# A convolution layer and a Mamba layer on one core: the Mamba's chunk grows from 512 to 1024 steps, in units that hold 64 channels and two time halves

## The chip, the core and the metric

The kernel runs on one core of a Trainium2 chip. A core has a matrix engine (PE, also called TensorE, with its weight loads shown apart as PEld), three engines for elementwise work (DVE, ACT and POOL), a queue that issues DMAs (SP), a working memory of 128 partitions (SBUF) and a small accumulation memory that PE writes (PSUM). The metric is the time of the program on the device in microseconds (us); lower is better. Each engine runs its own list of instructions in the order in which the program wrote them, and engines wait for each other through semaphores.

## What is computed

The input is 16 samples of 64 x 64 positions with 96 channels. Layer 0 normalizes, upsamples by a Fourier series, applies two dense layers with a polynomial between them, filters and downsamples, and is added to its input. Layer 1 normalizes and applies a Mamba block to the 4096 positions of a sample as one sequence; it too is added to its input. Cut to the Mamba:

```python
xz = einsum('blc,ec->ble', u, W_in); xs, z = split(xz, 2)        # 192 channels each
xc = silu(sum(xp[:, k:k + L, :] * conv_w[:, k] for k in range(3)) + conv_b)
dbc = einsum('bld,ed->ble', xc, W_x)                             # dt (6), B (16), C (16)
delta = softplus(einsum('blr,dr->bld', dt, W_dt) + b_dt)
dA  = exp(delta[..., None] * A)                                  # 192 channels x 16 states
dBu = delta[..., None] * Bm[:, :, None, :] * xc[..., None]
# for each step t:  h = dA_t * h + dBu_t ;  y_t = sum over states of h * C_t
y = (ys + xc * D) * silu(z)
out = einsum('bld,cd->blc', y, W_out)
```

Everything is float32, but for B, which is split into three bfloat16 parts that PE adds up again.

## The kernel before

The samples form a pipeline. While the Mamba works on sample s, the engines also do the steps of layer 0 for later samples: "S" steps (statistics and the first resampling), "W" steps (upsampling W_up, dense layers W_f and W_2, downsampling W_dn) and "D" steps (the last resampling, which also gives the input of the Mamba). A planner (`level`, `even`, `stage_rows`, with PE costs in `PE_US`) spreads these steps over the slots of a sample, and every engine's program is then written slot by slot by `run`: first the Mamba's unit of that slot, then its smaller parts, then the layer 0 steps that are due, each engine some slots behind PE (`LAG`). The order is fixed when the program is built. All layer 0 steps and the Mamba's own matrix steps (X, Z, DBC, DT, OUT) share three PSUM banks in turn (`cb`, `RING`).

The Mamba goes through a sample in 8 chunks of T = 512 steps. The recurrence runs on 128 partitions, which hold 32 channels times 4 states. A chunk thus has 24 units (6 groups j of 32 channels, 4 groups q of states), and a unit is one slot. For each unit:

- ACT makes `av` = exp(A x delta) from `rep_d` (L1008); `rep_d` and `rep_u` are delta and delta x xc, copied four times over the partitions by DMA from DRAM scratch.
- PE spreads B of one state group over the partitions into the bank `pb` (`spread_b`, L846), once for three units.
- DVE multiplies three strips of `rep_u` with `pb` into three PSUM banks `b3` (L1134), and then scans the three units one by one (L1140): `hs` = av x h + b.
- POOL multiplies `hs` with C, `cs` (L1181), and keeps the last state (L1185).
- PE adds up the four states of a channel into `py`, three strips of 32 partitions at once (`reduce`, L855).

After four state groups ACT copies `py` out (L1051), and POOL adds xc x D and multiplies with silu(z) (L1230, L1233). A chunk later PE makes OUT from that (`out`, L837 and L838). Two chunks ahead (`LEAD` = 2) the inputs are prepared: X (the convolution as three matmuls on shifted data, L810), Z (L816), DBC (L820), DT (L825), ACT's silu and softplus, the delta store to DRAM, POOL's multiply delta x xc (L1218), the deltax store, and the loads of `rep_d`, `rep_u` and `cs`. The table `AT` says in which slot of a chunk each part stands. WARM (L710) are matmuls without use that `warm` places in groups of slots with little PE work.

The broadcast for the next three units waits for DVE's multiply, since `pb` is a single buffer; DVE's multiply waits for the scans before it, since `b3` is:

```python
pe.wait_ge(dve_bu, count(dve_bu, G * NG + g))      # spread_b, PE
dve.wait_ge(pe_b, count(pe_b, G * NG + g + 1))     # unit, DVE: the multiply
dve.wait_ge(dve_h, count(dve_h, G * NU + n))
```

Of the kernel before, what the change touches and what calls it, by code (L numbers as in the profile page):

```python
# [13 lines left out]
L = HH * WW  # L14
# [7 lines left out]
T = 512  # L22
NC8 = L // T
NJ, NQ = DI // 32, DSTATE // 4
NU = NJ * NQ
NG = NU // 3
NHC, NAV, NHS = 6, 8, 6
XB_H = 8
LEAD = 2
# [4 lines left out]
BATCH = 8  # L34
# [8 lines left out]
LAG = {"pe": 0, "act": 4, "dve": 3, "pool": 1, "sp": 1, "bn": 3}  # L43
UNRINGED = ("SLD", "WLD", "DLD", "DW", "WARM")
# [24 lines left out]
def d_steps():  # L69
# [4 lines left out]
S_LAST, W_FIRST, W_LAST, D_FIRST, D_LAST = 87, 105, 87, 100, 139  # L74
X_AT, Z_AT, DBC_AT, DT_AT = (8, 10), (12, 11), 14, 18
KEEP_FREE = tuple(range(9, 9))

PE_US = {"ST": 0.45, "SA": 0.70, "SB": 0.70, "W_up": 0.70, "W_f": 0.71, "W_2": 2.10, "W_dn": 0.75, "D_lo": 1.20, "D_hi": 1.20,
         "X": 2.72, "Z": 0.92, "DBC": 1.82, "DT": 0.50, "OUT": 2.70, "WARM": 0.215}
PE_PB, PE_RED = 0.22, 1.00  # L80

WARM_TO = 4.8
# [4 lines left out]
def even(steps, lo, hi):  # L87
    free = [p for p in range(lo, hi + 1) if p % NU not in KEEP_FREE]
    return [(free[i * len(free) // len(steps)], st) for i, st in enumerate(steps)]


def loads(lo, hi, rows):

    load = {}
    for p in range(lo, hi + 1):
        load[p] = PE_PB * (p % 3 == AT["pe"]["pb"]) + PE_RED * ((p - AT["pe"]["red"]) % 3 == 0)
    for p, st in rows:
        if lo <= p <= hi:
            load[p] += PE_US.get(st[0], 0.2)
    return load  # L100


def level(steps, lo, hi, rows):
# [3 lines left out]
    for p in range(lo, hi + 1):  # L107
        groups.setdefault((p - 1) // 3, []).append(p)
    for limit in range(300, 1200, 5):
        out, todo = [], list(steps)  # L110
        for slots in groups.values():
            room = limit / 100 * len(slots) / 3 - sum(load[p] for p in slots)
            share = room / len(slots)
            for i, p in enumerate(slots):
                while (todo and p % NU not in KEEP_FREE and room >= PE_US[todo[0][0]] / 2
# [8 lines left out]
def warm(rows):  # L124
    load = loads(0, NC8 * NU - 1, rows)
    out = []
    for p in range(3, NC8 * NU, 3):
        short = WARM_TO - load[p] - load[p - 1] - load[p - 2]
        out += [(p, ("WARM", p, i)) for i in range(int(short / PE_US["WARM"]))]
    return out  # L130


def mamba_rows(k, z_only=False):
    at = k * NU
    rows = [(at + Z_AT[t], ("Z", k, t)) for t in range(2)]
    if not z_only:
        rows += [(at + X_AT[t], ("X", k, t)) for t in range(2)] + [(at + DBC_AT, ("DBC", k))]
        rows += [(at + DT_AT, ("DT", k, t)) for t in range(2)]
    return rows


def stage_rows(s, w_head, w_tail, d, beside=()):
# [20 lines left out]
def plan_of(kind):  # L163
    rows = []
    for k in range(NC8):
        if kind != "last" or k < NC8 - LEAD:
            rows += mamba_rows(k)
        elif k == NC8 - LEAD:
            rows += mamba_rows(k, True)
        rows.append((k * NU + OUT_AT, ("PAD", -1) if kind == "first" and k == 0 else ("OUT", k)))  # L170
    if kind == "last":
        rows.append((NC8 * NU + OUT_AT, ("OUT", NC8)))
        return padded(rows)
    rows = stage_rows(kind != "tail", kind != "tail", True, True, rows) + rows
# [1129 lines left out]
```

## Time and profile before

| | |
|---|---|
| median of 3 runs | 6343.44 us (6342.52 to 6347.34) |
| profiled execution, span from its first to its last instruction | 6343.7 us |
| PE busy, DVE busy, POOL busy, ACT busy | 6036.5, 5685.5, 5209.8, 5097.3 us |
| DVE scans (3072) | 3257.8 + 466.9 us |
| DVE multiplies (1024) | 1803.5 us |
| POOL multiplies with C (3072) | 3835.6 us |

The first 330 us prepare the first sample; from then on the recurrence runs without a break to the end, 16 samples after each other. The last two samples have less layer 0 work beside them. Busy time is not the same as being the bound: an engine may be busy with work for which nobody waits. The rows that say who waits for whom stand below.

### The profile page before, as it was taken

To read this page: it belongs to the slowest core of one execution; us is meant where nothing else is said; L and a number is where in the kernel's file an instruction comes from. 1 tells how busy PE (TensorE), PEld (TensorE's weight loads), DVE (VectorE), ACT (ScalarE), POOL (GpSimd) and SP (SyncE) were. 2 spreads that over 40 slices of the span, in tenths; PEclk is the share of its full clock that TensorE was granted. 3 is DMA by queue.
4 is the path that set the end of the run, shared out by engine and by line. 5 is a ranking of instruction groups with operands and counts; after the bars stand their busy time and mean duration, and the time that the engine had idled before them with its cause. 6 is when DMAs were issued, how large, how long until landed. Compare 5 with 4: busy or idle time off the path is not lost. (4 is left out here: it accounts for less than half of the span.)

```text
span 6343.7 us, 99100 instructions
## 1 busy us (share of the span) xinstructions
PE 6036.5 (95%) x32260; PEld 3123.0 (49%) x32260; DVE 5685.5 (90%) x4459; ACT 5097.3 (80%) x8658; POOL 5209.8 (82%) x5092
## 2 busy tenths in 40 slices
PE   8999999999999999999999999999999999998776
PEld 5645445454554545545455544545455454554222
DVE  0089999999999999999999999999999999999998
ACT  4588888888888888888888788888888888887664
POOL 0078888888888888888888888888888888888988
PEclk9999999999999999999999999999999999998665
DMA  3367676676767667675676767667676766767553
GB/s 95 88 165 170 160 167 157 163 162 169 169 154 168 155 165 170 155 182 142 167 162 162 173 156 169 155 164 163 167 169 156 166 154 165 168 142 160 129 124 75
DMA packets 805826, 983.25 MB, mean 155 GB/s; under 512 B 391258, under 2 KB 417542, under 8 KB 805318
## 3 DMA queue, kind: packets, MB, share of 16 engines
q1 hardware_dynamic: 805318, 976.92, 65.4%
q8 instruction: 265, 4.34, 0.3%
q14 instruction: 243, 1.99, 0.1%
HBM read 717.71 MB, written 259.00 MB: 154 GB/s over the span
## 5 line engine op out<-in xcount | busy, mean ns | idle before, releaser
L1181 POOL TENSOR_TENSOR hc<-hs,cs 128x512 f32<-128x512 f32 x3072 | 3835.6, 1271 | 692.7 <-DVE hs L1140 505.6
L1140 DVE TENSOR_TENSOR_SCAN hs<-av,state,b 128x512 f32<-128x512 f32 x2688 | 3257.8, 1263 | 88.6 <-POOL state L1185 4.9
L1008 ACT ACTIVATE av<-rep_d,nega 128x512 f32<-128x512 f32 x3072 | 2096.7, 713 | 41.5 <-DVE hs L1140 36.8
L1134 DVE TENSOR_TENSOR b<-rep_u,pb 128x1536 f32<-128x1536 f32 x1024 | 1803.5, 1761 | 211.0 <-PE pb L846 124.7
L855 PE MATMUL py<-hc,rsel 128*32 128x512 f32 x6144 | 1141.6, 634 | 40.6 <-POOL hc L1181 39.7
L769 PE MATMUL cb<-xu,w1a 96*128 96x392 f32 x2400 | 984.3, 513 | 27.7 <-DVE b1a L1120 17.4
L774 PEld LDWEIGHTS cb<-w2c,g 128*98 128x98 f32 x9600 | 885.9, 167 | 169.7 <-issue 106.9
L774 PE MATMUL cb<-w2c,g 128*98 128x96 f32 x9600 | 910.7, 252 | 17.4 <-ACT g L956 9.3
L956 ACT ACTIVATE g<-cb,b1a 128x392 f32<-128x392 f32 x1200 | 679.5, 579 | 87.0 <-PE cb L769 78.8
L810 PE MATMUL cb<-xn,wtap 96*96 96x512 f32 x1536 | 723.3, 607 | 2.4 <-ACT xn L1029 2.4
L769 PEld LDWEIGHTS cb<-xu,w1a 96*128 96x128 f32 x2400 | 414.5, 191 | 415.4 <-issue 199.3
L846 PE MATMUL pb<-bc,selb 96*128 96x512 bf16 x1024 | 406.6, 397 | 140.5 <-DVE b L1134 140.4
L1140 DVE TENSOR_TENSOR_SCAN hs<-av,zero_state,b 128x512 f32<-128x512 f32 x384 | 466.9, 1264 | 11.8
L949 ACT ACTIVATE vr<-cb 98x384 f32<-98x384 f32 x400 | 194.9, 487 | 320.2 <-PE cb L774 318.2
L810 PEld LDWEIGHTS cb<-xn,wtap 96*96 96x96 f32 x1536 | 243.5, 166 | 400.4 <-issue 380.0
L855 PEld LDWEIGHTS py<-hc,rsel 128*32 128x32 f32 x6144 | 157.2, 110 | 455.7 <-POOL hc L1181 225.0
L1218 POOL TENSOR_TENSOR dlt<-dlt,xcs 96x1024 f32<-96x1024 f32 x128 | 301.8, 2358 | 68.5 <-DMA delta_scratch<-dlt 68.5
L846 PEld LDWEIGHTS pb<-bc,selb 96*128 96x128 bf16 x1024 | 103.7, 101 | 508.1 <-issue 246.3
L763 PE MATMUL cb<-up_h,t1r 128*96 128x196 f32 x1600 | 345.7, 339 | 7.7 <-DMA t1r<-t_scratch 7.5
L837 PE MATMUL cb<-wo,xcs 96*128 96x96 f32 x2048 | 341.0, 292 | 3.7 <-POOL xcs L1233 3.5
L1233 POOL TENSOR_TENSOR xcs<-xcs,zs 96x512 f32<-96x512 f32 x256 | 324.1, 1266 | 20.1
L837 PEld LDWEIGHTS cb<-wo,xcs 96*128 96x128 f32 x2048 | 291.5, 205 | 86.0 <-issue 49.5
(109 smaller groups left out, 6703.4 us busy)
## 6 DMA issues: line engine op xcount, KB each, us to landing
rep_d<-delta_scratch SPq DMA_DIRECT2D x512, 384.0 KB, 7.0
rep_u<-deltax_scratch SPq DMA_DIRECT2D x512, 384.0 KB, 6.3
cs<-c_scratch SPq DMA_DIRECT2D x512, 256.0 KB, 5.9
delta_scratch<-dlt SPq DMA_DIRECT2D x128, 384.0 KB, 3.1
deltax_scratch<-dlt SPq DMA_DIRECT2D x128, 384.0 KB, 9.2
t1r<-t_scratch SPq DMA_DIRECT2D x160, 240.0 KB, 6.5
v_scratch<-v2s SPq DMA_DIRECT2D x192, 192.0 KB
xb<-in_x SPq DMA_DIRECT2D x128, 192.0 KB, 4.6
```

What stands on the lines that cost most here:

```text
L763: mm = pe.matmul(bank[0:C, e * 2 * GH:(e + 1) * 2 * GH], t1r[:, m % 2, i2 % 5, :], up_h[:, :], start=True, stop=True)
L769: mm = pe.matmul(bank[:, 0:BC], w1a[:, 128 * f:128 * f + 128], xu[:, b % 2, :], start=True, stop=True)
L774: mm = pe.matmul(bank[0:GH, C * j:C * j + C], g2[:, b % 2, f, GH * j:GH * j + GH], w2c[:, f, :], start=(f == 0), stop=(f == NF - 1))
L810: mm = pe.matmul(bank[0:C, :], wtap[:, tap, t, :], xn[:, k2 % 2, tap:tap + T], start=(tap == 0), stop=(tap == 2))
L837: pe.matmul(o, xcs[:, p, t, tb], wo[:, t, :], start=(t == 0), stop=False)
L846: pe.matmul(pb[:, :], selb[:, g % NQ, :], bc3[:, k % 4, :], start=True, stop=True).then_inc(pe_b, 1)
L855: mm = pe.matmul(py[32 * j:32 * j + 32, :], rsel[:, :], hc[:, (3 * g + j) % NHC, :], start=(q == 0), stop=(q == NQ - 1), skip_group_check= ...
L956: act.activation(g2[:, b % 2, f, :], bank[:, 0:BC], ACT.Square, bias=b1a[:, f:f + 1]).then_inc(fr, 1)
L1008: act.activation(av[:, n % NAV, :], rep_d[:, k % 2, j, :], ACT.Exp, scale=nega[:, q, j:j + 1])\
L1134: dve.tensor_tensor(b3[:, :, :], rep_u[:, k % 2, 3 * hf:3 * hf + 3, :], pb[:, None, :].broadcast_to([128, 3, T]), ALU.mult).then_inc(dve_b ...
L1140: dve.tensor_tensor_scan(hs[:, n % NHS, :], av[:, n % NAV, :], b3[:, n % 3, :], start, ALU.mult, ALU.add)\
L1181: pool.tensor_tensor(hc[:, n % NHC, :], hs[:, n % NHS, :], cs[:, k % 2, g % NQ, :], ALU.mult)\
```

## The change

The Mamba now goes in chunks of 1024 steps, four to a sample, and prepares one chunk ahead (`LEAD` = 1). A tile of prepared data (xc, z, delta, y) has 64 channels on each half of the partitions: steps 0 to 511 of the chunk on partitions 0 to 63, steps 512 to 1023 on partitions 64 to 127. There are three such tiles instead of two of 96 channels. X, Z and DT are now two matmuls side by side in the columns of PE's array, one for each time half; DBC, OUT and B's broadcast are two matmuls side by side in its rows. In the recurrence a unit still holds 32 channels times 4 states, but 1024 steps, so there are 24 units to 1024 steps in place of 48, and a unit takes two slots.

B's broadcast goes into `ub`, two buffers of 1024 steps, once for each unit, and DVE multiplies `rep_u` into it in place, unit by unit. The sum over states adds four strips at once (two units, two time halves). WARM is gone. `rep_d` and `rep_u` are loaded in three jobs a chunk of two units' data each, `cs` in four, one for each state group, with a single buffer. The rings of `av`, `hs` and `hc` hold four units of 1024 steps in place of 8, 6 and 6 of 512.

```diff
-T = 512
-NC8 = L // T
+TC = 512
+T = 2 * TC
...
-NHC, NAV, NHS = 6, 8, 6
+NHC, NAV, NHS = 4, 4, 4
-LEAD = 2
+LEAD = 1
...
-OUT_AT = 20
+OUT_AT = 9
 AT = {
-    "pe": dict(pb=1, red=5),
-    "act": dict(xn=10, y=(18, 6), d=11, mid=23, batch=16),
+    "pe": dict(red=6),
+    "act": dict(xn=5, d=10, batch=17, delta=27, mid=30, fin=36, y=(24, 40, 8)),
     "dve": dict(),
-    "pool": dict(u=23, bc=(18, 22), y=(17, 8)),
-    "sp": dict(rd=(1, 2, 3, 4), ru=(7, 9, 11, 13), cs=(15, 16, 17, 18), dl=21, du=4, x1=21, out=23),
+    "pool": dict(bc=(24, 30), u=32, y=(20, 36, 4)),
+    "sp": dict(x1=1, dc=23, dl=29, du=36, out=18, rd=((33, 0), (46, 0), (13, 1)), ru=((39, 0), (2, 1), (17, 1)),
+               cs=((40, 0), (44, 0), (47, 0), (3, 1))),
 }
...
-X_AT, Z_AT, DBC_AT, DT_AT = (8, 10), (12, 11), 14, 18
+Z_AT, X_AT, DBC_AT, DT_AT = (12, 13, 14), (9, 10, 11), 18, (22, 23, 24)
...
+            def spread_b(G, u):
+                if u == 0:
+                    pe.wait_ge(act_bc, count(act_bc, G + 1))
+                pe.wait_ge(dve_h, count(dve_h, G * NU + u - 1))
+                for h in range(2):
+                    part = slice(64 * h, 64 * h + 48)
+                    mm = pe.matmul(ub[:, u % 2, TC * h:TC * h + TC], selb[part, u // 2 % NQ, :], bc3[part, G % 2, :],
+                                   start=True, stop=True)
+                mm.then_inc(pe_b, 1)
...
+            def reduce(G, g):
+                t, q = g // NQ, g % NQ
+                pe.wait_ge(pool_hc, count(pool_hc, G * NU + 2 * g + 2))
+                if q == 0:
+                    pe.wait_ge(act_y, count(act_y, G * NP + t))
+                for h in range(2):
+                    for j in range(2):
+                        strip = 32 * (2 * h + j)
+                        mm = pe.matmul(py[strip:strip + 32, :], rsel[:, :], hc[:, (2 * g + j) % NHC, TC * h:TC * h + TC],
+                                       start=(q == 0), stop=(q == NQ - 1), skip_group_check=True)
+                mm.then_inc(pe_red, 1)
...
+                dve.wait_ge(pe_b, count(pe_b, G * NU + u + 1))
+                dve.tensor_tensor(ub[:, u % 2, :], rep_u[:, jobs % 2, u % 2, :], ub[:, u % 2, :], ALU.mult)\
+                    .then_inc(dve_bu, 1)
+                if u % 2 == 0:
+                    dve.wait_ge(pool_st, count(pool_st, G * NG + u // 2 + 1 - NHS // 2))
+                dve.wait_ge(dve_bu, count(dve_bu, G * NU + u + 1))
+                dve.wait_ge(act_a, count(act_a, G * NU + u + 1))
```

On PE, in the middle of a chunk before, around the two X steps: `pb` is B's broadcast, `cb<-xn,wtap` X, `cb<-xn,winz` Z, `py` the sum over states, `xb` and `vr` belong to layer 0.

```order
L846 MATMUL pb<-bc,selb 128x512
L855 MATMUL py<-hc,rsel 32x512 x3
L742 MATMUL cb<-xb,up_w 100x384
L810 MATMUL cb<-xn,wtap 96x512 x3
L846 MATMUL pb<-bc,selb 128x512
L810 MATMUL cb<-xn,wtap 96x512 x3
L855 MATMUL py<-hc,rsel 32x512 x3
L816 MATMUL cb<-xn,winz 96x512
L742 MATMUL cb<-xb,up_w 100x384
L816 MATMUL cb<-xn,winz 96x512
L846 MATMUL pb<-bc,selb 128x512
```

The same place after the change; ahead of these rows stand the broadcast for unit 5 (`ub`) and three more quarters of OUT (`cb<-wo,xcs` and `cb<-ident,x1o`), each like the first two rows:

```order
L886 MATMUL cb<-wo,xcs 128x96 x6
L890 MATMUL cb<-ident,x1o 128x96 x2
L846 MATMUL cb<-xn,wtap 64x512 x6
L915 MATMUL py<-hc,rsel 32x512 x4
L846 MATMUL cb<-xn,wtap 64x512 x6
L903 MATMUL ub<-bc,selb 128x512 x2
L776 MATMUL cb<-xb,up_w 100x384
L846 MATMUL cb<-xn,wtap 64x512 x6
L797 MATMUL cb<-up_h,t1r 96x196 x2
L854 MATMUL cb<-xn,winz 64x512 x2
L903 MATMUL ub<-bc,selb 128x512 x2
```

OUT, which stood ten slots behind the X steps, now stands directly ahead of them, and the broadcasts of units 6 and 7 stand between the second and third X and behind the first Z.

On DVE, at the border of two chunks before (`b` is the product of rep_u and B, `hs` the scan, `spare` belongs to a filling step):

```order
L1140 SCALAR_TENSOR_TENSOR hs<-av,state,b 128x512 [waits act_a,dve_bu,pool_st]
L1140 SCALAR_TENSOR_TENSOR hs<-av,state,b 128x512 [waits act_a] x2
L1100 COPY spare<-cb 96x1 [waits pe_conv]
L1134 TENSOR_TENSOR b<-rep_u,pb 128x1536 [waits dve_h,pe_b,ru_ld0]
L1140 SCALAR_TENSOR_TENSOR hs<-av,zero_state,b 128x512 [waits act_a,dve_bu,pool_st]
```

The same place after the change:

```order
L1177 COPY spare<-cb 96x1 [waits pe_conv]
L1210 TENSOR_TENSOR ub<-rep_u,ub 128x1024 [waits pe_b,ru_ld0]
L1217 SCALAR_TENSOR_TENSOR hs<-av,zero_state,ub 128x1024 [waits act_a,dve_bu,pool_st]
L1210 TENSOR_TENSOR ub<-rep_u,ub 128x1024 [waits pe_b]
L1217 SCALAR_TENSOR_TENSOR hs<-av,zero_state,ub 128x1024 [waits act_a,dve_bu]
```

Multiply and scan now alternate, each multiply waits for PE's broadcast (pe_b), and none waits for the scans before it (dve_h).

On SP, where the transfers for a coming chunk are issued, before (`x1c` is the input of X and Z, `rep_u`, `rep_d` and `cs` feed the recurrence):

```order
L659 DMA rep_d<-delta_scratch 32x6x512
L513 DMA t1r<-t_scratch 128x5x96 [waits pe_conv]
L662 DMA rep_u<-deltax_scratch 32x6x512 [waits du_st,dve_bu]
L662 DMA rep_u<-deltax_scratch 32x6x512 x3
L576 DMA v_scratch<-v2s 2x64x384 [waits cb_free1]
L666 DMA cs<-c_scratch 32x4x512 [waits dc_st,pool_hc]
L666 DMA cs<-c_scratch 32x4x512 x3
L605 DMA x1c<-x_scratch 96x512 [waits x1_st0,x1_st1,act_xn]
```

After (`xn` is now loaded directly):

```order
L666 DMA rep_u<-deltax_scratch 32x2x1024 [waits du_st,dve_bu]
L666 DMA rep_u<-deltax_scratch 32x2x1024 x3
L585 DMA v_scratch<-v2s 2x64x384 [waits cb_free2]
L698 DMA cs<-c_scratch 32x1024 [waits dc_st,pool_hc]
L698 DMA cs<-c_scratch 32x1024 x3
L698 DMA cs<-c_scratch 32x1024 [waits dc_st,pool_hc]
L698 DMA cs<-c_scratch 32x1024 x3
L522 DMA t1r<-t_scratch 128x5x96 [waits pe_conv]
L666 DMA rep_d<-delta_scratch 32x2x1024 [waits dl_st,act_a]
L666 DMA rep_d<-delta_scratch 32x2x1024 x3
L698 DMA cs<-c_scratch 32x1024 [waits dc_st,pool_hc]
L698 DMA cs<-c_scratch 32x1024 x3
```

The next row after these is the load of `xn`; the first `rep_u` here is that of the chunk which begins next, where before it was that of the chunk after next.

## Rows read from the trace of the kernel before

**Rows 1.** The page: span, busy time and share of each engine.

```profile
span 6343.7 us, 99100 instructions
...
PE 6036.5 (95%) x32260; PEld 3123.0 (49%) x32260; DVE 5685.5 (90%) x4459; ACT 5097.3 (80%) x8658; POOL 5209.8 (82%) x5092
```

**Rows 2.** 375 us in mid-run: busy PE, PEld, DVE, ACT, POOL; granted clock, DMA share, GB/s.

```profile
1083.00:1458.00 375.00, 368.34 (x2016) 191.28 (x2015) 354.01 (x278) 316.20 (x541) 325.05 (x318) 1.00 0.70 164
```

**Rows 3.** DVE in order of time: start, length, line, operation, count.

```profile
2505.96 1.76 DVE L1134 TENSOR_TENSOR b<-rep_u,pb 128x1536 f32<-128x1536 f32 x1
2507.81 3.63 DVE L1140 TENSOR_TENSOR_SCAN hs<-av,state,b 128x512 f32<-128x512 f32 x3
2511.54 1.76 DVE L1134 TENSOR_TENSOR b<-rep_u,pb 128x1536 f32<-128x1536 f32 x1
```

**Rows 4.** DVE's waits: total us, times, longest us.

```profile
DVE b L1134 <- PE pb L846: 124.7, 182, 3.4
```

**Rows 5.** Scans: shortest/median/longest ns, first and last start in us.

```profile
L1140 DVE TENSOR_TENSOR_SCAN hs<-av,state,b x2688: 1248/1256/1283, 386.9 to 6326.3; 128x512 f32<-128x512 f32 x192
L1140 DVE TENSOR_TENSOR_SCAN hs<-av,zero_state,b x384: 1248/1256/1282, 330.0 to 6013.6; 128x512 f32<-128x512 f32 x192
```

**Rows 6.** Groups by line: busy us, mean ns of one | idle before, releaser.

```profile
L1113 DVE BATCH_NORM_STATS2 bst<-x1s 96x6 f32<-96x512 f32 x128 | 85.3, 666 | 51.7 <-ACT x1s L965 51.7
```

**Rows 7.** The same view, POOL's multiplies of 512 and of 1024 steps.

```profile
L1230 POOL TENSOR_TENSOR xcs<-xcs,yv 96x512 f32<-96x512 f32 x256 | 325.8, 1273 | 2.7 <-ACT yv L1051 2.7
L1218 POOL TENSOR_TENSOR dlt<-dlt,xcs 96x1024 f32<-96x1024 f32 x128 | 301.8, 2358 | 68.5 <-DMA delta_scratch<-dlt 68.5
```

**Rows 8.** PE in order of time around X; a matmul counts as two half passes.

```profile
2518.79 2.74 PE L810 MATMUL cb<-xn,wtap 96*96 96x512 f32 x6
2521.37 0.38 PE L846 MATMUL pb<-bc,selb 96*128 96x512 bf16 x1
2521.58 2.74 PE L810 MATMUL cb<-xn,wtap 96*96 96x512 f32 x6
2524.25 1.06 PE L855 MATMUL py<-hc,rsel 128*32 128x512 f32 x6
2525.24 2.26 PE L816 MATMUL cb<-xn,winz 96*96 96x512 f32 x4
```

**Rows 9.** PE in order of time around one W_dn.

```profile
2504.05 0.87 PE L780 MATMUL cb<-vr,dn_h 98*64 98x384 f32 x4
2504.84 0.33 PE L747 MATMUL cb<-mv,gavg 96*96 96x1 f32 x2
```

**Rows 10.** PE in order of time: OUT's first row and what follows it.

```profile
2497.23 0.61 PE L837 MATMUL cb<-wo,xcs 96*128 96x96 f32 x4
...
2499.91 0.38 PE L846 MATMUL pb<-bc,selb 96*128 96x512 bf16 x1
```

**Rows 11.** SP: four issues, DMAs with KB and us to landing, one wait.

```profile
2519.80 2.64 SPq L662 DMA_DIRECT2D rep_u<-deltax_scratch  x4
...
rep_u<-deltax_scratch SPq DMA_DIRECT2D x512, 384.0 KB, 6.3
delta_scratch<-dlt SPq DMA_DIRECT2D x128, 384.0 KB, 3.1
deltax_scratch<-dlt SPq DMA_DIRECT2D x128, 384.0 KB, 9.2
...
SPq L648 <- DMA deltax_scratch<-dlt: 432.1, 86, 9.0
```

**Rows 12.** WARM matmuls; the last sample's stretch; PE in it, in order.

```profile
L710 PE MATMUL py<-selb 96*32 96x512 bf16 x673 | 160.2, 381 | 0.0
...
5964.00:6327.00 363.00, 259.07 (x818) 88.17 (x817) 350.14 (x262) 217.17 (x326) 322.29 (x315) 0.62 0.47 108
...
6052.70 1.17 PE L837 MATMUL cb<-wo,xcs 96*128 96x96 f32 x4
...
6057.93 0.63 PE L846 MATMUL pb<-bc,selb 96*128 96x512 bf16 x1
```

More of the change, by code:

```diff
@@ L87, in even @@
 def even(steps, lo, hi):
-    free = [p for p in range(lo, hi + 1) if p % NU not in KEEP_FREE]
+    free = list(range(lo, hi + 1))
     return [(free[i * len(free) // len(steps)], st) for i, st in enumerate(steps)]
@@ L121, in level, with mamba_rows @@
     raise ValueError("the steps find no place")
[L124 to L138, printed above, removed]
+def mamba_rows(k, z=True, ahead=True):
+    at = k * NS2
+    rows = []
+    if ahead:
+        rows += [(at + X_AT[t], ("X", k, t)) for t in range(NP)]
+    if z:
+        rows += [(at + Z_AT[t], ("Z", k, t)) for t in range(NP)]
+    if ahead:
+        rows += [(at + DBC_AT, ("DBC", k, h)) for h in range(2)]
+        rows += [(at + DT_AT[t], ("DT", k, t)) for t in range(NP)]
     return rows
@@ L152, in stage_rows @@
         rows += [(S_LAST + 4, ("WLD", 0)), (W_FIRST - 3, ("WG", 0))] + even(w[:2], W_FIRST - 8, W_FIRST - 6)
-        rows += level(w[2:W_HEAD], W_FIRST, NC8 * NU - 1, rows + list(beside))
+        rows += level(w[2:W_HEAD], W_FIRST, SL - 1, rows + list(beside))
     return rows
@@ L456, in iteration @@
                 for k in chunks:
-                    for n in range(NU):
-                        if units and k < NC8:
+                    for n in range(NS2):
+                        if units and k < NC:
                             unit_fn(st.s, k, n)
                         c_fn(st, k, n)
-                        if not (last and k + LEAD >= NC8):
+                        if not (last and k + LEAD >= NC):
                             a_fn(st, k, n)
-                        while todo and when(todo[0]) <= k * NU + n:
+                        while todo and when(todo[0]) <= k * NS2 + n:
                             step_fn(st, todo.pop(0)[1])
@@ L675, in c_part @@
+                if n == at["out"] and not (G < 1):
+                    k1, s1 = (k - 1) % NC, st.s + (k - 1) // NC
+                    for h in range(2):
+                        i = st.at[("OUT", k, h)]
+                        sp.wait_ge(cb_free[i % RING], st.freed(i))
+                        sp.sem_inc(sp_passed, 1)
+                        sp.dma_start(tok(otok, s1, k1 * T + h * TC, TC), os_[:, h]).then_inc(out_st, 16)
+                if n == at["out"] and k < NC and not (G < 0):
                     load_x1o(st.s, k)
@@ L877, in _ @@
+                late = n + NS2 - AT["pe"]["red"]
+                if late < NS2 and late % 4 == 0 and not (G < 1):
+                    reduce(G - 1, late // 4)
             run(lambda row: row[0], unit, step, lambda st, k, n: None, c_part, setup)
```

622 lines of the change are left out of this document (325 added, 297 removed).

## The prediction

> **What bounds the kernel now.** I began with the page: PE is busy 95% of the span, DVE 90% [rows 1]. A busy PE need not be the bound, so I cut whole samples out of the middle: in 375 us DVE works 354, PE 368, at a granted clock of 1.00 [rows 2]. DVE's order of time decides between the two: one multiply of 1536 steps, three scans, the next multiply 5.58 us after the last (1.76 + 0.09 + 3.63 + 0.10), with no wait inside [rows 3]. So DVE's own work is the floor. Its list of waits names the one thing that lifts time above it: the multiply waits 124.7 us for PE's broadcast of B [rows 4]. The execution adds up: first scan at 330.0, last one over at 6326.3 + 1.3 = 6327.6 [rows 5]; between them 1024 x 5.58 = 5714 of floor, 124.7 of waiting, 159 of statistics and small things (the rest; the statistics alone are 0.67 us each, rows of one kind x128 [rows 6]); then 16.1 to the end. Sum 6343.7, the span, and the median of the runs is 6343.44, so a sum against the span needs no correction.
>
> **DVE's new floor.** A unit is now 1024 steps: one multiply and one scan. No row has these lengths, so each price has two ends. Multiply: two thirds of 1.76 are 1.17; and between statistics over 512 elements at 0.67 [rows 6] and the multiply over 1536 at 1.76 lie 1024 elements and 1.09 us, so 512 fewer make 1.21. I take 1.23, since statistics write next to nothing. Scan: two thirds of three scans' 3.63 are 2.42 [rows 3]; one scan of double length saves the start between two, about 0.1, so 2.33, at most 2.43. The gap between multiply and scan stays at 0.09, since the scan waits for its own multiply as before. The gap behind the scan should go: the multiply no longer waits for the scan before it (the order shows no dve_h on it), and three scans without such a wait last 3.63 instead of 3 x 1.26, an overlap of 0.08 at each of two borders [rows 3, 5]. I take 1.23 + 0.09 + 2.33 - 0.08 = 3.57, with ends 3.50 (multiply 1.17) and 3.85 (scan 2.43, gap of 0.10 kept; less what the pile below then loses, 390 us more). 1536 x 3.57 = 5484, which is 230 less than 5714. With 330, 159 and 16.1 unchanged (head and tail keep their steps but for some tiny loads) the sum without waits is 5989.
>
> **What the change takes from other engines** lies beside DVE and I count it at nothing. ACT and POOL lose per-instruction starts (POOL's 1024-step form is 2.36, two of 512 are 2.54 [rows 7]); ACT is busy 80% of the span and POOL 82% [rows 1]. PE loses work: per 1024 steps, X goes from 12 passes of 0.86 to 9 pairs, the sums from 16 of 1.0 to 12, Z, DBC and DT from 4 passes to 3 pairs, while the broadcast grows from 16 single matmuls to 24 pairs [rows 8]. This holds if pairs on separate column halves run together; they do so now in W_dn, where four half passes of 384 columns take 0.79 us to the next instruction, against 4 x 0.32 one by one (an X half pass of 512 takes 0.43 [rows 8, 9]). So PE is lighter on average. Average is not what ends a wait here.
>
> **Where the floor is lost: the pile on PE.** B's broadcast for unit u+1 goes into the buffer in which unit u-1's product stood, so PE may write it only when scan u-1 is over, and DVE needs it when unit u is over. Between two broadcasts PE therefore has at most two units, 7.14 us. Before, OUT and the two X stood apart, with a broadcast between any two of them. Now the order shows between the broadcasts of units 5 and 6, in every chunk: OUT for 1024 steps, X, a sum, X. Count from the chunk's first multiply. Scan 3 is over at 4 x 3.57 = 14.3, the broadcast of unit 5 takes 0.3 (0.21 from [rows 8], and about 0.1 for the change of tile shape: the sum's two passes of 0.43 take 0.99 there). OUT also waits for the last third of y: POOL does it behind the product of unit 2, that is 10.7 + 2.36 + 1.27 + 1.27 = 15.6 [rows 7]. OUT before is 2.69 for 24 half passes, 0.112 each [rows 10]; now 64. If the two halves of rows go together that is 40 x 0.112 = 4.5, if not 64 x 0.112 = 7.2; no row shows row halves, the column halves of [rows 9] speak for together, and I take 5.0. Then X 2.6, sum 1.0, X 2.6, broadcast 0.3 [rows 8]: 15.6 + 11.5 = 27.1. DVE has been done with unit 5 since 21.4. **Stall 5.7 us.** Before the next broadcast stand the third X, W_up (0.7: four half passes of 196 columns at X's rate) and Z (0.86): 2.6 + 0.7 + 0.86 + 0.3 = 4.5 against 3.57, 0.9 more; then PE is level. 6.6 us a chunk, in 63 of 64 chunks: **416 us**. Ends: 4.2 (OUT 4.5, no wait for y, no second stall) and 8.8 (OUT 7.2): 265 to 554.
>
> The row says that a change of tile shape costs about 0.1 us. The Trainium skill, in TensorEngine Tiling (Array Packing), Key Properties, states that changing the tiling mode drains the TensorE; it speaks against this change, in which nearly every PE instruction stands beside one of another shape. Row and rule agree; without the pile's five such borders the sum would be 63 x 0.5 = 30 us lower, 6500.
>
> **Other waits.** The 124.7 us before come from groups in which PE is a little late; elsewhere PE has 6 to 7 us of work in each two units by the order, so I keep half, 62 (0 to 125). **Transfers:** product and next chunk now lie within one chunk. The deltax store can go when POOL has multiplied three times behind unit 17, at about 70 us; it then lands in 3.1 (what the delta store takes) to 9.2, four issues take 2.6 and rep_u lands in 6.3 [rows 11]: 82 to 88, and unit 24 begins at 85.7. (The stall above moves both alike.) Behind it in SP's queue stand cs, rep_d, cs, and only then xn, for which ACT waits ahead of its next exponentials; today's queue has SP waiting 432 us for the deltax store without hurting DVE, because that store is a chunk ahead [rows 11]. I take 1 us a chunk, 63 (0 to 4 each, 252).
>
> **Sum:** 5989 + 416 + 62 + 63 = **6530**, 2.9% above 6343.7. No change would need all waits together at 355, 5.6 a chunk.
>
> **Rivals.**
> *The floor wins (faster).* If OUT's two row halves hide each other's weight loads too, OUT for 1024 steps costs the 2.7 of one OUT before, y is ready by then, and the broadcast of unit 6 is done at 14.6 + 2.7 + 2.6 + 1.0 + 2.6 + 0.3 = 23.8 against 21.4: 2.5 a chunk, 5989 + 158 + 62 = 6209. For it: pairs of column halves do run together [rows 9]. Against: 64 half passes must then take the time of 24, and X alone twice is 5.2 of 7.14. It decides below 5.6 a chunk.
> *PE's clock falls (slower).* The filler matmuls are gone; before there were 673 of them, and in the stretch without them the clock was 0.62 of full (half speed, 1.2 GHz, for much of it), OUT took 5.23 instead of 2.69 [rows 12]. If each pile begins at half speed, OUT's 40 steps cost 40/24 x 2.54 = 4.2 more: 6530 + 63 x 4.2 = 6795. For it: four groups with little PE work ahead of one of the four piles. Against: three of four piles follow dense work. The Trainium skill names this in TensorE: Matmul & The Clock Gate, HAM oscillation: waits between bursts of matmuls bring the lower clock back. The row of the last stretch agrees.
> *Late transfers (slower).* 4 us a chunk instead of 1: 6719.
> *In place costs double (slower).* The multiply reads and writes one PSUM bank, which no row shows; before it read one and wrote another. At half rate it costs 1.07 more: 1536 x 1.07 = 1643, less 63 x 2.1 at the pile: 8040.
> *The change doesn't do what it says (slower).* If four strips don't run together as three do, each of 768 sums takes 1.9 instead of 1.0, and PE, already near 7 us per two units, becomes the bound; with a fifth of it finding room, 6530 + 0.8 x 768 x 0.9 = 7080.
>
> **How the numbers follow.** Forecast 0.63, floor 0.16, clock 0.06, transfers 0.08, in place 0.04, strips 0.03. Within 0.2% is about what measurement can tell from no change. Of the forecast's 0.63 its low end gives 0.02 to faster and 0.03 to same; the floor rival is faster throughout. Faster 0.18, same 0.03, slower 0.79. Range 6220 to 6820: below it lies some 0.10 (most of the floor rival), above it some 0.11 (in place, strips, the top of the forecast).
>
> **What would show it.** Right: DVE's waits put 300 to 500 us on the multiply for PE, nearly all on units 6 and 7 of each chunk; multiply near 1.23, scan near 2.33, pairs of them 3.57 apart elsewhere; OUT 4.5 to 5.5 us long. Wrong: the multiply well over 1.3 (in place), sums over 1.1 (strips), a granted clock below 0.95 in mid-sample (clock), DVE waiting for rep_u or av (transfers), or DVE's waits for PE under 200 us (the floor wins).

## The result, and the profile after

The changed kernel takes **7996.47 us** (median of 4 runs, 7967.36 to 8004.99) against 6342.98 before: a ratio of 1.2597, interval 1.2574 to 1.2621. Slower, as forecast, but the forecast was 6530 and its range ended at 6820. The profiled execution spans 8001.2 us. The runs of this kernel lie within 38 us of each other, so in the experiments, which are single runs, a smaller difference says nothing.

The page: no engine is busy all the time any more, PE least of all compared with [rows 1], and its granted clock (tenths of full, 40 slices) is below 9 nearly everywhere.

```profile
span 8001.2 us, 101956 instructions
...
PE 6590.0 (82%) x36195; PEld 3216.6 (40%) x36195; DVE 5568.4 (70%) x3441; ACT 4513.5 (56%) x6604; POOL 4596.4 (57%) x3108
...
PEclk9888978788797887878789788887978888787555
```

The groups of DVE and of the sum (count | busy us, mean ns | idle before, releasers):

```profile
L1210 DVE TENSOR_TENSOR ub<-rep_u,ub 128x1024 f32<-128x1024 f32 x1536 | 1867.8, 1216 | 2037.0 <-PE ub L903 1963.5 <-DMA rep_u<-deltax_scratch 71.1
L1217 DVE TENSOR_TENSOR_SCAN hs<-av,state,ub 128x1024 f32<-128x1024 f32 x1152 | 2703.1, 2346 | 85.4 <-ACT av L1073 10.3 <-DVE ub L1210 2.2 <-issue 0.9
L915 PE MATMUL py<-hc,rsel 128*32 128x512 f32 x6144 | 1013.2, 738 | 408.7 <-POOL hc L1260 309.5 <-ACT yv L1122 95.7
```

DVE's instructions cost what was forecast (1.216 and 2.346 us; forecast 1.23 and 2.33). Nearly all the loss is one entry: the multiply waits 1963.5 us for PE's broadcast, where [rows 4] had 124.7 and the forecast 416 + 62. The lists of waits (us, times, longest) name a second one, on ACT, that the kernel before doesn't have:

```profile
DVE ub L1210 <- PE ub L903: 1963.5, 557, 18.0
...
ACT xn L1094 <- DMA xn<-x_scratch: 894.1, 63, 23.7
```

The four chunks of one sample (columns as in [rows 2]): DVE works 81 to 93 us in each, about its floor, and PE's clock is far from [rows 2]'s 1.00.

```profile
3253.00:3370.00 117.00, 102.54 (x570) 49.27 (x571) 87.12 (x55) 71.69 (x106) 71.31 (x47) 0.87 0.60 132
3370.00:3487.00 117.00, 92.38 (x507) 40.33 (x505) 86.15 (x53) 68.02 (x98) 72.01 (x49) 0.81 0.54 125
3487.00:3625.00 138.00, 113.82 (x612) 59.97 (x612) 93.23 (x62) 69.93 (x105) 74.48 (x51) 0.76 0.61 136
3625.00:3743.00 118.00, 103.19 (x574) 51.00 (x573) 81.09 (x47) 71.75 (x105) 69.55 (x47) 0.87 0.50 112
```

**Where in a chunk.** I took DVE's time between the end of a scan and the next multiply from the order of time (it includes the few statistics that stand there) and averaged it over the 56 chunks of the samples in the middle. Of 33.0 us a chunk, 14.0 stand ahead of units 2 to 4, 10.5 ahead of units 6 and 7 (7.4, 7.8, 19.2 and 7.7 in the four chunks of a sample), 5.2 ahead of units 12 to 15, 3.2 elsewhere. Only the second place was forecast, at 6.6.

The first place, in the second chunk of a sample, in order of time (ACT, PE, DVE):

```profile
3372.35 0.49 ACT L1010 ACTIVATE vr<-cb 98x384 f32<-98x384 f32 x1 [0.63 <-PE cb L808]
3386.47 0.20 ACT L1094 ACTIVATE xn<-xn 96x2 f32<-96x2 f32 x1 [13.63 <-DMA xn<-x_scratch]
...
3387.71 0.47 ACT L1010 ACTIVATE t1s<-cb 100x384 f32<-100x384 f32 x1
...
3375.36 0.93 PE L803 MATMUL cb<-xu,w1a 96*128 96x392 f32 x2
3388.23 1.60 PE L776 MATMUL cb<-xb,up_w 64*100 64x384 f32 x2 [11.95 <-ACT t1s L1010]
3389.76 2.98 PE L803 MATMUL cb<-xu,w1a 96*128 96x392 f32 x4
3392.67 0.61 PE L903 MATMUL ub<-bc,selb 48*128 48x512 bf16 x2
...
3378.84 2.35 DVE L1217 TENSOR_TENSOR_SCAN hs<-av,state,ub 128x1024 f32<-128x1024 f32 x1
3393.32 1.23 DVE L1210 TENSOR_TENSOR ub<-rep_u,ub 128x1024 f32<-128x1024 f32 x1 [12.14 <-PE ub L903]
```

ACT stands 13.63 us in front of xn. Behind that wait stands its eviction of t1s, for which PE waits 11.95 us, and when PE goes on it does so at half clock (0.93 us for two matmuls before, 2.98 for four after). DVE has waited 12.14 us when the broadcast comes. The second place in the third chunk, on PE: OUT (L886, L890), X (L846), the sum, one D step, X, and the broadcast that DVE waits for.

```profile
3524.09 0.91 PE L886 MATMUL cb<-wo,xcs 64*128 64x96 f32 x12 [2.26 <-issue]
...
3530.80 1.60 PE L886 MATMUL cb<-wo,xcs 64*128 64x96 f32 x12
3532.33 1.17 PE L890 MATMUL cb<-ident,x1o 96*128 96x96 f32 x4
3533.43 5.39 PE L846 MATMUL cb<-xn,wtap 96*64 96x512 f32 x12
3538.75 1.26 PE L915 MATMUL py<-hc,rsel 128*32 128x512 f32 x8
...
3541.22 2.80 PE L846 MATMUL cb<-xn,wtap 96*64 96x512 f32 x12
3543.95 0.39 PE L903 MATMUL ub<-bc,selb 48*128 48x512 bf16 x2
```

The same quarter of OUT takes 0.91 and 1.60 us, the same X 5.39 and 2.80: half clock for some 13 of the 20 us. And OUT begins late: over the samples in the middle 3.7 us behind the multiply of unit 4, against 0.0 to 0.6 in the other three chunks. PE stands 2.26 us in front of it, until 0.09 us after DVE's small step `b1a`, which reads one of the shared banks and has its place behind a scan in DVE's list.

### The profile page after: what moved, and what is told of

Its sections match the earlier page's. It is cut to its first block and busy times, and to the rows that moved or that the text cites. A ratio compares the mean times of both kernels' runs of the same rounds, so it can differ in the third digit from the quotient of the medians.

```text
span 8001.2 us, 101956 instructions
## 1 busy us (share of the span) xinstructions
PE 6590.0 (82%) x36195; PEld 3216.6 (40%) x36195; DVE 5568.4 (70%) x3441; ACT 4513.5 (56%) x6604; POOL 4596.4 (57%) x3108
## 5 line engine op out<-in xcount | busy, mean ns | idle before, releaser
L1260 POOL TENSOR_TENSOR hc<-hs,cs 128x1024 f32<-128x1024 f32 x1536 | 3618.6, 2356 | 2583.5 <-DVE hs L1217 2530.7
L1210 DVE TENSOR_TENSOR ub<-rep_u,ub 128x1024 f32<-128x1024 f32 x1536 | 1867.8, 1216 | 2037.0 <-PE ub L903 1963.5
L1217 DVE TENSOR_TENSOR_SCAN hs<-av,state,ub 128x1024 f32<-128x1024 f32 x1152 | 2703.1, 2346 | 85.4 <-ACT av L1073 10.3
L1073 ACT ACTIVATE av<-rep_d,nega 128x1024 f32<-128x1024 f32 x1536 | 1736.8, 1142 | 170.7 <-DVE hs L1217 168.1
L1217 DVE TENSOR_TENSOR_SCAN hs<-av,zero_state,ub 128x1024 f32<-128x1024 f32 x384 | 901.0, 2346 | 26.3 <-ACT av L1073 1.7
L903 PE MATMUL ub<-bc,selb 48*128 48x512 bf16 x3072 | 667.2, 433 | 163.6 <-DVE hs L1217 162.6
L846 PE MATMUL cb<-xn,wtap 96*64 96x512 f32 x2304 | 584.6, 646 | 0.0
L797 PEld LDWEIGHTS cb<-up_h,t1r 128*96 128x96 f32 x1600 | 258.3, 182 | 378.1 <-issue 195.9
L1289 POOL TENSOR_TENSOR xcs<-xcs,yv 128x512 f32<-128x512 f32 x192 | 243.5, 1268 | 279.9 <-ACT yv L1122 279.8
L886 PE MATMUL cb<-wo,xcs 64*128 64x96 f32 x3072 | 281.0, 326 | 32.6 <-issue 27.7
```

Of the source, the lines that this page charges most:

```text
L797: mm = pe.matmul(bank[0:C, e * 2 * GH:(e + 1) * 2 * GH], t1r[:, m % 2, i2 % 5, :], up_h[:, :], start=True, stop=True)
L846: mm = pe.matmul(bank[64 * h:64 * h + 64, :], wtap[:, tap, :, :].rearrange("c t p -> c (t p)")[:, own], xn[:, G2 % 2, TC * h + tap:TC * h ...
L886: pe.matmul(cb[:, (i + h) % RING, C * b:C * b + C], xcs[half, (G - 1) % 2, j, 128 * b:128 * b + 128], wo[half, j, :], start=(j == 0), stop ...
L903: mm = pe.matmul(ub[:, u % 2, TC * h:TC * h + TC], selb[part, u // 2 % NQ, :], bc3[part, G % 2, :], start=True, stop=True)
L1073: act.activation(av[:, u % NAV, :], rep_d[:, jobs % 2, j, :], ACT.Exp, scale=nega[:, q, at:at + 1])\
L1210: dve.tensor_tensor(ub[:, u % 2, :], rep_u[:, jobs % 2, u % 2, :], ub[:, u % 2, :], ALU.mult)\
```

## The experiments

Four theories stood at the start: **A**, the late load of xn; **B**, half clock; **C**, the pile of OUT and X, as forecast; **D**, ub released too late. **P** (PE has no room on average), **Q** (less work, more half clock) and **L** (lockstep) came later.

**e1: xn earlier.**

```diff
-                if n == at["x1"]:
+                if n == at["x1"] and G2 == 0:
                     load_xn(s2, k2)
+                if n == 45 and G2 + 1 < NS * NC:
+                    load_xn(*divmod(G2 + 1, NC))
```

> Only the load of xn is issued earlier: at slot 45 of the chunk before, ahead of the second rep_d job and the third cs job, instead of slot 1. Theory A (ACT stands in its queue before xn until the load lands, 63 waits of 14 us, 894.1 us in all; the evictions behind it are late, so PE and the broadcasts for units 2 to 4 are): DVE's idle time ahead of units 2 to 4, 13.9 us a chunk, goes almost whole, 63 x 13 = 820, so 7180 us, and up to 300 lower if PE then keeps its clock, so 6880 to 7200; ACT's wait for xn under 100 us. Theory B (PE at half clock is the cause, and the wait for xn only fills time that PE would lose anyway): the idle time moves on to units 6 and 7, 7700 us or more, and the clock stays near 0.82. Theory C (the pile of OUT and X is the cause, as forecast): at most the waits ahead of units 2 to 4 shrink by half, 7500 or more.

The time was 7622.06 us, and ACT's wait was still 393.1. Half of the wait went and 374 us with it: A has a share, but the time lies above its range, in that of C.

**e2: X, Z, DBC, DT and what follows two slots later** (`X_AT` = 11, 12, 13; `OUT_AT` stays 9).

> X, Z, DBC, DT and everything made from them stand two slots later, so that the broadcast of unit 6 lies between OUT and X. Theory A (late xn): X is not held up by the late load any less, the waits at units 2 to 4 stay at 14 us a chunk, only a part of the pile (units 6 and 7, 10.5 us a chunk) goes: 63 x 5 = 315, so 7680, between 7550 and 7850. Theory C (the pile): the 10.5 us at units 6 and 7 fall to 3 and the chain behind them catches up, 63 x 7.5 = 470 or more, 7520 or less. Theory B (half clock): 7850 to 8050, since PE's work is the same.

The time was 8159.56 us, above the range of every theory. Units 6 and 7 lost most of their wait outside the third chunk (0.4 to 0.6 and 2.0 to 2.6), but it came back at units 0, 3, 8 and 11. That speaks against C as stated.

**e3: product into hs, scan in place there; the broadcast waits for the multiply (dve_bu), not for the scan.**

> The product is written into hs and the scan runs in place there, so PE may write the next broadcast as soon as the multiply two units before is over, 2.4 us earlier than now. Theory D (the short release of ub is what makes DVE and PE wait for each other): every late broadcast gains up to 2.4 us; DVE's 557 waits for PE shrink by 2.4 each at most, 1300 us, and at least by PE's own waits for the scan, 162.6 us: 6700 to 7500. Theories A, B and C: waits of 7 to 18 us a piece are hardly shorter, 63 x 2 piles x 2.4 = 300, so 7600 to 7850. If the in-place form itself had cost the multiply or the scan anything, 1.22 and 2.35 us would fall; no theory here expects that.

The time was 8940.86 us: a scan took 3.19 us instead of 2.35, and POOL's copy of the state 1.65 instead of 0.19. All four theories missed this; it needed e7.

**e4: the kernel before without fillers** (`WARM_TO = 0.0`).

> The kernel before without its 673 filling matmuls (160 us of PE). Theory B (the fillers held the clock, and PE's clock falls without them whatever else is done): the granted clock falls below 0.90, DVE's waits for PE grow from 125 to 400 us or more, 6600 to 7000. Theories A, C and D (the clock falls in the changed kernel because PE stands idle behind ACT or in the ping-pong with DVE): the clock stays above 0.93 and the time within 6300 to 6420.

The time was 6355.15 beside 6350.33 us, and the clock 0.945 beside 0.966. In the kernel before, the fillers held up 0.02 of the clock and no time.

**e5: xn earlier still** (slot 36; 45 where the chunk begins a sample).

> The load of xn is issued at slot 36 of the chunk before (slot 45 only where the chunk begins a sample), 9 slots or some 17 us earlier than in the first experiment, where ACT still waited 393.1 us for it (6 us in two chunks of four, 14 in one). Theory A (what ACT waits for xn comes back in the time almost one to one): ACT's wait for xn under 100 us, 7622 - 300 = 7320, between 7200 and 7400. Theory AB (PE's idle time behind ACT also costs it the clock, so that every stall is paid twice): the share of half clock falls with it, granted clock over 0.90, 6900 to 7200. Theory P (PE's own work, 355 us a sample at full clock against DVE's 353, leaves no room, and PE's remaining waits and half clock come from its ping-pong with DVE): 7400 or more.

The time was 7568.07 us at clock 0.844, in the range of P; ACT's wait is 0.8 us in all. Taking the whole wait of 894 us away gives back 428. Units 2 to 4 fell from 14.0 to 5.6 us, and units 6 and 7 rose from 10.5 to 12.4: in the second chunk of a sample the 12 us ahead of unit 3 went, and 13.5 stand ahead of unit 6, where some 6 stood. There OUT now waits 1.4 us for POOL's last third of y, and then takes 9.8 us instead of 5.7, at half clock for much of it.

Other waits of PE come into view. Its list between 400 and 7000 us (over its whole span the kernel before has 29.1 for xb, 17.4 for b1a, 7.5 for t1r and none for xt):

```profile
PE cb L773 <- DMA xb<-in_x: 74.2, 13, 6.2
PE cb L888 <- DVE b1a L1199: 53.9, 14, 3.9
PE cb L830 <- DMA xt<-xt_scratch: 51.4, 15, 5.4
PE cb L799 <- DMA t1r<-t_scratch: 44.4, 14, 4.0
```

Three of the four are loads of layer 0 from the same SP queue. In one sample of e11 (below), which has them as well, PE waits 5.72 us for xb ahead of the broadcast for unit 3 in the first chunk, and 3.63 and 3.22 us for xt and t1r ahead of that for unit 2 in the third; DVE then waits 5.99 and 7.78 us. No run took these waits away.

**e6: the late load put into the kernel before** (`load_x1c` at slot 5 of its own chunk for every second chunk).

> The kernel before, with the load of the layer input x1c of every second chunk of 512 issued at slot 5 of the chunk that needs it, instead of slot 21 of the chunk before; nothing else. That puts the changed kernel's late load into the kernel before, 64 times. Theory A (a late load that ACT waits for stops PE and with it DVE): ACT waits 8 to 15 us each time, and since PE there works 368 us of 376, nearly all of it is seen: 64 x 7 to 64 x 13, 6790 to 7180. With theory AB the granted clock falls too (under 0.92, from 0.965) and it is 7000 to 7500. Rival: the kernel before is deeper (8 units of av ahead, prepared two chunks ahead) and takes it in: under 6500.

The time was 6550.15 us beside 6342.41. The waits:

```profile
ACT xn L1031 <- DMA x1c<-x_scratch: 206.1, 64, 9.3
```

ACT waits less than expected (3.2 us each), and the time lies between the two ranges. But 206 us of waiting cost 208 us: in this kernel A's price, one to one, is right, with the clock nearly unmoved (0.955 against 0.966).

**e7: product in an SBUF buffer of its own** (`bu`; the scan reads it there, and the broadcast waits as in e3).

```diff
...
+                dve.wait_ge(dve_h, count(dve_h, G * NU + u))
-                dve.tensor_tensor(ub[:, u % 2, :], rep_u[:, jobs % 2, u % 2, :], ub[:, u % 2, :], ALU.mult)\
+                dve.tensor_tensor(bu[:, :], rep_u[:, jobs % 2, u % 2, :], ub[:, u % 2, :], ALU.mult)\
...
```

> The product is written into a buffer of its own in SBUF, neither in place in PSUM (as changed) nor in place in SBUF (as in e3, where the scan took 3.19 us instead of 2.35 and GpSimd's products 2.64 instead of 2.36). PE may write the next broadcast once the multiply two units before is over, 2.35 us sooner than in the changed kernel. Theory S (a scan whose inputs both lie in SBUF gets in GpSimd's way and is slowed by it): scan 3.0 us or more, 8600 or more. Theory I (it was the scan in place in SBUF that was slow): scan 2.35 to 2.55, GpSimd at 2.36. With I, theory D (the late release of ub makes the waits) gives 7850 or less; if the release does not matter, 1536 scans that are 0.1 to 0.2 longer give 8000 to 8250.

The time was 8949.76 us. DVE and POOL, groups:

```profile
L1219 DVE TENSOR_TENSOR_SCAN hs<-av,state,bu 128x1024 f32<-128x1024 f32 x1152 | 3499.2, 3038 | 76.2 <-ACT av L1074 2.4 <-issue 1.3 <-DVE bu L1212 0.9
...
L1262 POOL TENSOR_TENSOR hc<-hs,cs 128x1024 f32<-128x1024 f32 x1536 | 4048.5, 2638 | 1922.3 <-DVE hs L1219 1921.9 <-PE py L916 0.4
L1265 POOL COPY state<-hs 128x2 f32<-128x2 f32 x768 | 1239.5, 1614 | 0.0
```

The scan is not in place, and as slow as in e3: S, not I. Scans with POOL at work for less than a fifth of their time take 2.36 us, the others 3.2 to 3.7 in the mean and up to 4.5. The Trainium skill, SBUF — State Buffer, "SBUF: two separate sides", says that VectorE with two SBUF inputs and GpSimd lock each other out of a port for a whole instruction if GpSimd's reads SBUF; these rows agree, as a scan of 2.36 us that grows to 4.5 has gained about one POOL product (2.36 us in the changed kernel). So e3 and e7 say nothing on D, which stays open; with one operand in PSUM, before and after, there is no such price.

**e8: e5 and e2 together.**

> The load of xn as in e5_xn36, and X, Z, DBC and DT two slots later as in e2, so that a broadcast stands between OUT and X. With the late load gone, theory C (the pile) gives back what stands ahead of units 6 and 7, 9 us a chunk, without the late load taking it again: 350 to 550 below e5_xn36. Theory P (PE is the bound on average, so a pile that is spread out is paid in small pieces elsewhere): within 150 of e5_xn36, either side.

The time was 7637.31 us, 69 more than e5. C as stated falls again, P stands.

**e9: less work on PE, away from the pile** (each W_2 adds one of its three products; the other two are left out).

> As e5_xn36, but each W_2 step adds one of its three products instead of all three: two thirds of layer 0's second matrix product are left out, and what the kernel writes changes accordingly. That takes 400 of 600 small matmuls a sample from PE, 400 x 92 ns = 37 us of its 355 us at full clock. None of them stands in the piles at units 3, 6 and 12. Theory P (PE's work fills the whole sample, so a wait anywhere is paid again and again): at least the 37 us a sample come back, 16 x 37 = 590, 6980 or less. Theory C (single piles at fixed places hold DVE up, PE is idle enough elsewhere): 7400 or more. Theory Q (less work only means more idle time and so more of half clock): the share of half clock rises from 0.28 and the time stays above 7300.

The time was 7633.48 us at clock 0.785. PE lost some 35 us of work a sample (an estimate, its rows at their full-clock lengths) and nothing came back, against P; the signs of Q are met. By PE's rows of ten samples, 162 us a sample ran at half clock, in e5 103: much of what was saved went into slower matmuls.

**e10: fillers** (as WARM, but adding zero to the strips).

> As e5_xn36, with filling matmuls as the kernel before had them: one of 512 columns ahead of a broadcast and two ahead of a sum, wherever the strips of py are being added up (they add zero), 0.21 us each at full clock, about 130 a sample, 27 us of PE at most. Theory B (PE falls to half clock because it stands still in short waits): the granted clock rises from 0.844 to 0.93 or more, and since half clock costs 51 us a sample, the time falls by 16 x 10 to 16 x 30, 7100 to 7400. Theory P without B (the fillers only add work): the clock stays under 0.88 and the time rises by up to 16 x 27 = 430, 7600 to 8000.

The time was 7636.80 us at clock 0.891, a time in P's range at a clock between the two. Half clock fell from 129 to 88 us a sample and paid nothing; the likely reason, that the fillers took what it gave, isn't shown.

**e11: DT over 64 rows** (58 of them with zero weights).

```diff
...
-                        rows = slice(96 - 64 * h, 96 - 64 * h + RANK)
+                        rows = slice(64 - 64 * h, 128 - 64 * h)
...
```

> As e5_xn36, with DT's pairs of matmuls over 64 rows (58 of them zero weights) instead of the 6 rows that it needs; the number and length of matmuls stay. In e5 the clock halves in units 12 to 14 of most chunks, right after the DT pairs, though PE's records have no gap over 0.4 us there. Theory R (matmuls that use few rows of the array count little for the clock): the half clock at units 12 to 14 goes, its share of the span falls by a third, 7566 - 63 x 3 = 7370 or less. Theory not R (half clock there comes from the short gaps ahead of it): share and time unchanged, 7500 to 7620.

The time was 7463.76 us at clock 0.873, 104 less than e5: between the ranges of R and not R. PE in order of time at DT (L875), in e5:

```profile
2233.62 1.07 PE L875 MATMUL cb<-dbo,wdt 6*64 6x512 f32 x4
...
2237.65 1.30 PE L875 MATMUL cb<-dbo,wdt 6*64 6x512 f32 x4
2238.89 0.61 PE L905 MATMUL ub<-bc,selb 48*128 48x512 bf16 x2
2240.34 1.68 PE L805 MATMUL cb<-xu,w1a 96*128 96x392 f32 x2 [0.84 <-ACT xs L1012]
2241.94 1.94 PE L917 MATMUL py<-hc,rsel 128*32 128x512 f32 x8
```

and in e11:

```profile
2200.95 1.08 PE L875 MATMUL cb<-dbo,wdt 64*64 64x512 f32 x4
...
2204.99 1.08 PE L875 MATMUL cb<-dbo,wdt 64*64 64x512 f32 x4
2206.00 0.39 PE L905 MATMUL ub<-bc,selb 48*128 48x512 bf16 x2
2207.68 0.93 PE L805 MATMUL cb<-xu,w1a 96*128 96x392 f32 x2 [1.28 <-ACT xs L1012]
2208.53 1.06 PE L917 MATMUL py<-hc,rsel 128*32 128x512 f32 x8
```

The same matmuls at the same length (1.07, 1.08), but behind the third pair of 6 rows the next three steps take 1.6 to 1.8 times as long, and behind 64 rows they don't. Averaged over the samples, unit 13 ran some 85% of its time at half clock in the first chunk of e5, and none in e11. In 53 of the 56 chunks in the middle of e5 the clock fell between the first DT row and 3 us behind the last, in e11 in none. So the half clock there goes as R said, and gives back 104 us where R had at least 196 (7566 to 7370).

**e12: e11 with fillers where the plan is slack; e13: e11 with e2's slots; e14: both.**

> As e11_dt_rows, and filling matmuls (512 columns, adding zero to the open strips of py) ahead of sums, 113 a sample, laid where the plan gives PE less than 6.9 us in four slots: most of them in the slack stretch at the end of the second chunk and of the fourth. Theory B (the half clock that is left, 72.5 + 25.5 us a sample in e11, comes from the slack stretches before it): its share falls by half or more, granted clock 0.93 or more, 16 x 20 = 320 less than 7464, 7050 to 7250. Theory P (PE has no room, each filler costs its 0.21 us): 7500 to 7800 whatever the clock does.

> As e11_dt_rows, and X, Z, DBC and DT two slots later, so that a broadcast stands between OUT and X. With neither the late load nor the slow DT in the way, theory C (the pile of OUT and X costs what stands ahead of units 6 and 7, 11 us a chunk) gives 300 to 600 less than e11: 6860 to 7160. Theory P (the work of the pile is only met elsewhere, since all groups around it are full): within 150 of e11, 7310 to 7610.

> Both: fillers as in e12_warm and X two slots behind OUT as in e13_dt_apart. If B and C hold together, 6700 to 6950. If the pile's work only moves and the fillers only add, 7450 or more. In between, the parts add up as e12 and e13 show them alone.

The times were 7521.30, 7583.26 and 7563.57 us, against 7463.76: each is a little slower, as P had it, and the waits only change place.

**e15: less work on PE, in the pile** (two of X's three taps and two of OUT's three tiles are left out).

```diff
...
-                    for tap in range(3):
+                    for tap in range(1):
...
-                    for j in range(NP):
+                    for j in range(1):
...
```

> As e5_xn36, but X adds one of its three taps and OUT one of its three tiles of 64 channels: two thirds of X's and of W_out's products are left out, and what the kernel writes changes accordingly. That takes 30.5 us a sample of PE work at full clock (X 32.7 x 2/3, the product of OUT 13.05 x 2/3), somewhat less than e9 took (35), but all of it from the pile between the broadcasts of units 5 and 6 and the one behind it, 7.6 us of 15 in each chunk. Theory L (DVE and PE go in lockstep over two buffers: time is lost where PE has more work between two broadcasts than DVE has in two units, and slack elsewhere can't be saved up for it): where e9 gained nothing, this gains what stands ahead of units 6 and 7, 10 to 11 us a chunk in e5, at least 63 x 7 = 440: 7130 or less. Theory Q (PE with less work only falls to half clock more): 7450 or more, as in e9, with a clock under 0.82.

The time was 7063.74 us, 504 less than e5. DVE's waits for the broadcast, of e5, e9 and e15:

```profile
DVE ub L1212 <- PE ub L905: 1546.5, 503, 17.0
```

```profile
DVE ub L1211 <- PE ub L904: 1656.9, 486, 19.0
```

```profile
DVE ub L1212 <- PE ub L905: 1051.5, 474, 10.4
```

Ahead of units 6 and 7 the wait fell from 12.4 to 5.0 us a chunk. Some 30 us of PE work a sample out of the pile give 504 us; 35 us out of the rest give nothing. That fits L: PE may write a broadcast only when the scan of the unit before last is over, so it can't run ahead, and what it saves in one pair of units is idle time there, often followed by half clock. Time is then lost wherever work between two broadcasts exceeds two units.

e15 rules out that less work only means more half clock (Q): its clock rose to 0.851. L against P is less sure. What e15 gained is about the work it took out, as P would have it too, and e9, which speaks against P, was itself slowed by the clock. For L speaks that nearly all the gain stands at units 6 and 7, where the work was, and that in e5 PE is idle 52 us of the 453 of a sample. No run gave PE a third buffer, which would test L directly.

## Why the prediction was wrong

- **Floor: right.** In place costs nothing, four strips run together (1.06 us), unstalled units follow each other after 3.5 to 3.6 us. The rival "in place costs double" came to 8040, next to the result, and was false; a matching time would have misled without the row.
- **The pile: right in place; its size at full clock is in part luck.** Forecast 6.6 a chunk; 7.4 and 7.7 in the first and fourth chunk, which meet it at full clock. But OUT took 5.7 to 5.8 us instead of 5.0 (below), and it began 0.0 and 0.4 us behind the multiply of unit 4, not 1.3: it didn't wait for y there, since the stall at units 2 to 4 had given POOL the time. Where no stall stands ahead, in the second chunk of e5, it does wait. e15 shows that the pile is real.

```profile
2940.79 0.91 PE L888 MATMUL cb<-wo,xcs 64*128 64x96 f32 x12
...
2946.00 0.69 PE L892 MATMUL cb<-ident,x1o 96*128 96x96 f32 x4
2946.61 2.80 PE L848 MATMUL cb<-xn,wtap 96*64 96x512 f32 x12
```

  (PE in order of time in e11, first chunk of a sample: OUT from 2940.79 to 2946.61.)
- **Transfers: the step that failed first.** "I take 1 us a chunk, 63 (0 to 4 each, 252)" priced only DVE's wait for rep_u, of which there is none after the first. The working itself named xn, last in SP's queue, for which ACT waits, and gave that no price. It lands 13.8 us after its issue (median), and ACT waited 14.2 in each of 63 chunks. e5 puts its worth at 428 us, some seven of the fourteen a chunk: of DVE's 14.0 at units 2 to 4, 5.6 stay, and 1.9 more stand at units 6 and 7. The late loads of layer 0 (xb, xt, t1r: 170 us of PE's waits in e5) had no price either.
- **Clock: chance 0.06, reason false, size too small.** The rival rested on the missing fillers; in the kernel before they hold up no time (e4), and put into the changed kernel they give none back (e10, e12). Its "wrong if below 0.95" was met (0.823). Summed over PE's rows of ten samples, 291.7 us a sample ran at full clock, 116.4 at half, 75.1 were idle, against 368.4, 1.0 and 7.0 before. Half clock came behind stalls, slack stretches and DT. It is the larger part of what makes the third chunk's pile 19.2 instead of 7.5 us: OUT took 10.1 us there instead of 5.7 and the X behind it 5.3 instead of 2.8 (means), 6.9 together, and another 3.7 are OUT's late start behind `b1a`. The Trainium skill, TensorE: Matmul & The Clock Gate, "HAM oscillation", names the first of these (waits between bursts), and the half clock behind the 11.95 us wait above agrees; DT in e5 shows one without a wait of note (no gap over 0.24 us between its rows).
- **"So PE is lighter on average": hardly.** With its rows at their full-clock lengths (an estimate) its work is 355 us a sample, against 369 before with 10 of fillers. "I keep half, 62" assumed room outside the pile. The units next to it had none: what e2 moved out of the pile was met at units 0, 3, 8 and 11. Units 12 to 15 alone took 5.2 a chunk, of which e11 took 2.3 away with DT's half clock.

Of the 1466 us missing from the forecast, 428 are the late load (e5) and 104 DT's clock (e11). Of the other 934 I can say where they stand: DVE's waits in e11 are 24.0 us a chunk, where the forecast had 8.6, with 12.7 at units 6 and 7 and 5.6 at units 2 to 4. Slots and fillers don't give them back (e8, e12 to e14). The rows explain a part. At the pile of e11, half clock makes OUT and the X behind it 6.4 us longer in the second chunk of a sample and 6.9 in the third (OUT 9.9 and 10.4 us instead of 5.7, X 5.0 instead of 2.8), about 210 us in 16 samples if all of it reaches DVE, an estimate. One sample of e11 also shows what stands ahead of units 3, 2 and 6:

```profile
3042.35 1.06 PE L773 MATMUL cb<-ident,xb 128*96 128x128 f32 x4 [5.72 <-DMA xb<-in_x]
...
3248.61 1.14 PE L830 MATMUL cb<-xt,wtot 96*96 96x256 f32 x2 [3.63 <-DMA xt<-xt_scratch]
...
3254.24 1.59 PE L799 MATMUL cb<-up_h,t1r 128*96 128x196 f32 x4 [3.22 <-DMA t1r<-t_scratch]
...
3270.28 1.60 PE L888 MATMUL cb<-wo,xcs 64*128 64x96 f32 x12 [3.85 <-DVE b1a L1200]
```

How much of the rest is half clock and how much work without room isn't settled: but for e11, every run that raised the clock also added work, took it away or moved a wait.

## What to carry to other kernels

When a chunk is doubled, the steps that prepare it double, but the time between two turns of a double buffer need not; compare the largest run of work between two turns with that time, not the averages. A load that an engine waits for in its own queue costs what stands behind that wait on the engine, so price it by its place in the issuing queue even if its consumer is far from the critical path. Take work out of two different places by the same amount: the difference tells a bound from a window, as long as the clock is the same in both.

## What the runs showed of the hardware

- Around the matmuls of 6 rows the granted clock fell to half in 53 of 56 chunks (e5), with no gap over 0.24 us between PE's records up to the last of them; with 64 rows, the same count and length, it fell in none (e11).
- A scan with both inputs in SBUF took 3.04 us in the mean, 2.36 where POOL was hardly at work and up to 4.5 beside it, and POOL's copy of two columns 1.61 instead of 0.19 (e7); with one input in PSUM the scan took 2.35 whatever POOL did (the changed kernel).
- A multiply that reads and writes the same PSUM bank costs no more than one that doesn't: 1.216 us in place, 1.218 into SBUF (e7).
- Two loads of 384 KB in the same queue of the changed kernel landed after 13.8 us (xn, right behind rep_d and cs) and 6.8 us (x1o), medians.
